# Query, key and value projections as three rounded products each, in an attention and expert kernel on one core

## The reference

```python
q = split_heads(layernorm(x) @ wq.T + bq)      # 16 heads of 16
k = split_heads(ctx @ wk.T + bk)
v = split_heads(ctx @ wv.T + bv)
attn = softmax(einsum('bhqd,bhkd->bhqk', q, k) / sqrt(16))
x = x + merge(attn @ v) @ wo.T + bo
n = layernorm(x)
probs = softmax((n @ Wg + bg) / 5.0)           # 8 experts
vals, idx = top_k(probs, 2); gates = mask / (sum(mask) + 1e-9)
h = gelu(n @ W1[e] + b1[e]); out_e = h @ W2[e] + b2[e]
x = x + sum_e gates[e] * out_e
```

## Time and profile before

| | |
|---|---|
| median of 3 runs | 808.66 us |
| profiled execution, whole | 804.46 us |
| its span, first to last instruction | 802.4 us |
| attention, batches 0 to 7 | 40.9 to about 524 us |
| expert tiles | about 524 to 802.4 us |
| batches 2 to 5 | about 62 us each |
| mean granted clock of PE, share of full speed | 0.992 |

### The profile page before, as it was taken

How to read it: one execution, slowest core, us unless ns; L and a number is a source line. 1 busy time by engine, 2 the same in 40 slices (tenths; PEclk the granted TensorE clock), 3 DMA queues, 4 the chain that set the end, 5 groups by cost and what they waited for, 6 DMA issues and landing times.

```text
span 802.4 us, 16337 instructions
## 1 busy us (share of the span) xinstructions
PE 755.2 (94%) x4672; PEld 451.9 (56%) x4672; DVE 612.2 (76%) x1126; ACT 455.1 (57%) x663; POOL 393.9 (49%) x357
## 2 busy tenths in 40 slices
PE   9999999999999999999999898869999999999994
PEld 4443344444444444444444333349989888999994
DVE  6787778798697787788788787667777887776773
ACT  2066676776766766766676674854345443444441
POOL 6506143547637728728725613306553564444443
PEclk9999999999999999999999999999999999999998
DMA  7665857657666767757658467666454465454441
GB/s 226 208 179 176 228 165 226 209 179 250 206 188 239 213 198 234 190 188 250 186 174 268 149 178 260 257 241 161 89 101 80 79 145 93 74 84 70 72 69 12
DMA packets 90660, 136.24 MB, mean 170 GB/s; under 512 B 15456, under 2 KB 49216, under 8 KB 90192
## 3 DMA queue, kind: packets, MB, share of 16 engines
q1 hardware_dynamic: 76592, 117.33, 48.0%
q0 software_dynamic: 13296, 17.09, 12.1%
q10 hardware_dynamic: 688, 0.79, 0.3%
HBM read 71.25 MB, written 64.04 MB: 169 GB/s over the span
## 4 chain that ended last, share of the span: by engine, by line
PE 71%; DMA 7%; DVE 7%; ACT 6%; issue 5%; SPq 2%; POOL 1%; POOLq 0%; DVEq 0%; another core or an unknown queue 0%
PE ps_pv L1568 13%; PE ring L1555 10%; PE ring L1734 9%; PE ring L1716 8%; PE ring L1542 7%; PE ps_x L1599 7%; ACT probs L1041 4%; PE ps_x L1619 4%; DMA out<-y_sb,xs 3%; PE ps_x L1609 3%; PE ring L1725 3%; DVE negm L1113 2%; PE ps_x L1629 2%; DMA den<-oT 2%; PE ps_pv L1707 1%
## 5 line engine op out<-in xcount | busy, mean ns | idle before, releaser
L1113 DVE TENSOR_REDUCE negm<-ring 128x2 f32<-128x1024 f32 x256 | 310.2, 1222 | 73.0 <-PE ring L1542 65.0
L1041 ACT ACTIVATE probs<-ring 128x1024 f32<-128x1024 f32 x256 | 260.0, 1024 | 91.7 <-PE ring L1555 79.4
L922 POOL DMA_INDIRECT out<-y_sb,xs x71 | 110.2, 1553 | 152.3 <-DMA out<-y_sb,xs 73.6
L1568 PE MATMUL ps_pv<-probs,v_aug 128*32 128x512 f32 x1024 | 136.8, 606 | 4.0 <-ACT probs L1041 3.9
L1555 PE MATMUL ring<-kq 64*128 64x512 f32 x512 | 125.4, 491 | 7.5 <-DVE negm L1113 7.3
L1542 PE MATMUL ring<-kq 64*128 64x512 f32 x512 | 105.9, 412 | 10.6 <-ACT probs L1041 5.4
L1555 PEld LDWEIGHTS ring<-kq 64*128 64x128 f32 x512 | 47.4, 183 | 108.5 <-issue 72.4
L1074 ACT CAST xsT_hi<-ps_pv 128x256 fp32r<-128x256 f32 x70 | 26.1, 373 | 133.8 <-PE ps_pv L1707 122.9
L1734 PE MATMUL ring<-w_hi,hT_hi 128*128 x284 | 85.3, 300 | 0.1
L815 POOL DMA_INDIRECT xs_dram<-xg,rows x64 | 63.3, 988 | 39.9 <-issue 15.9
L1734 PE MATMUL ring<-w_lo,hT_hi 128*128 x284 | 80.0, 282 | 0.0
(11 more groups left out here) (197 smaller groups left out, 1223.4 us busy)
## 6 DMA issues: line engine op xcount, KB each, us to landing
kq<-k_dram SPq DMA_DIRECT2D x64, 192.0 KB
kq<-q_dram SPq DMA_DIRECT2D x64, 192.0 KB
xs<-xs_dram SPq DMA_DIRECT2D x71, 132.5 KB
k_dram<-qk_hi SPq DMA_DIRECT2D x32, 256.0 KB
q_dram<-qk_hi SPq DMA_DIRECT2D x32, 256.0 KB, 2.8
o_dram<-oT SPq DMA_DIRECT2D x32, 256.0 KB
w_dram<-w_sb SPq DMA_DIRECT2D x12, 512.0 KB
w_hi<-w_dram SPq DMA_DIRECT2D x12, 512.0 KB, 7.4
```

The lines of the kernel that those rows point to most:

```text
L922: pool.indirect_dma_start(out=out, out_offset=bass.IndirectOffsetOnAxis(ap=xs[j % AHEAD][:, TOKEN:TOKEN + 1].bitcast(I32), axis=0), in_=y_ ...
L1041: nc.scalar.activation(probs[kt][:, 2 * jp:2 * jp + 2, :], ring[PLACE["ST", u, p] % RINGS][:], ACT.Exp).then_inc(exp_done, 1)
L1113: nc.vector.tensor_reduce(negm[:, v % 2, :, jp, kt], ring[PLACE["MX", v, p] % RINGS][:], AX.X, ALU.max, negate=True).then_inc(max_free, 1)
L1568: mm = nc.tensor.matmul(ps_pv[2 * DH * j:2 * DH * (j + 1), :], v_aug[:, kt, HPG * g + j, :], probs[kt][:, j, :], start=(kt == 0), stop=(kt ...
```

## The change

1. **Three rounded products.** For batches 1 to 7 every projection is `high*high + high*low + low*high` in float32r. Batch 0, which is projected ahead of the loops, stays float32.
2. **Who makes the parts.** ACT rounds the three weight matrices once. XT: ACT casts `ps_x` to `xn_hi` in place of the copy to xnT, then DVE takes `ps_x - xn_hi` to `xn_lo`, and only that frees the bank. Context: ACT rounds it in two halves (`high_kv`, rounds (3,3) and (3,4)), POOL takes the difference (`low_kv`).
3. **Memory.** The low parts lie over the whole ones, kvT has one buffer, the descriptor ring of POOL's transfers is 8192 in place of 16384 bytes a partition, and a scatter waits until the one two before it has landed.
4. **Moves.** XT0 of batch i+2 goes from round (2,7) to (2,6); the second staged cast from (3,2) to (3,5); the context load of batch i+2 on SP from the start of the batch to behind the weight load near its end; on POOL the first low part of a staged weight from ahead of the scatters to behind `ln2`, and Q1's split ahead of `ln`.

```diff
-NEXT = {(2, 7): "XT0", (3, 1): "XT1"}
+NEXT = {(2, 6): "XT0", (3, 1): "XT1"}
+XT_LOW = {(2, 7): "XT0", (3, 2): "XT1"}
+KV_HIGH = {(3, 3): 0, (3, 4): 1}
-STAGE_SLOTS = {(1, 2): 0, (3, 2): 1}
+STAGE_SLOTS = {(1, 2): 0, (3, 5): 1}
...
             def load_kv(b):
-                if b > 1:
-                    sp.wait_ge(full["V1"], b - 1)
-                sp.dma_start(kvT[:, b % 2], ctx_kv[b]).then_inc(kv_in, 16)
+                sp.wait_ge(full["V1"], b)
+                sp.dma_start(kvT[:], ctx_kv[b]).then_inc(kv_in, 16)
...
                 more = i + 1 < B
-                if i + 2 < B:
-                    load_kv(i + 2)
...
                 if i == 0:
                     load_w1(E - 2)
+                if i + 2 < B:
+                    load_kv(i + 2)
                 if more:
                     put_max(i + 1, 0)
...
+            def scatter_tile(b, k, t):
+                n = NT * (TOPK * b + k) + t
+                if n >= 2:
+                    pool.wait_ge(scattered[n % 2], 16 * (n // 2))
                 pool.indirect_dma_start(out=xs_dram, ...
+            def low_kv(b):
+                pool.wait_ge(kv_split, 3 * b - 1)
+                nc.gpsimd.tensor_tensor(kv_lo[:], kvT[:], kv_hi[:].bitcast(F32), ALU.subtract).then_inc(kv_split, 1)
...
                 if i + 1 < B:
                     split("K", i + 1, 0)
                     split("Q", i + 1, 0)
+                    split("Q", i + 1, 1)
                 if i + 2 < B:
                     ln(i + 2)
                 if i + 1 < B:
-                    split("Q", i + 1, 1)
                     split("K", i + 1, 1)
-                if i in STAGED:
-                    low_staged(i, 0)
                 if i > 1:
                     scatter(i - 2, NP * (NG * i + 1) + SCATTER if i < B - 1 else None)
                 if i > 0:
                     ln2(i - 1)
-                if i + 2 < B:
-                    add_bo(i + 2)
+                if i in STAGED:
+                    low_staged(i, 0)
                 if i + 1 < B:
                     for g in range(3):
                         place_v(i + 1, g)
+                if i + 2 < B:
+                    low_kv(i + 2)
+                    add_bo(i + 2)
                 if i in STAGED:
                     low_staged(i, 1)
...
-                if kind == "XT":
-                    if b > 0:
-                        act.wait_ge(full["Q1"], b)
+                if kind == "XT" and b == 0:
                     nc.scalar.copy(xnT[:, int(name[2]), :], ps[:]).then_inc(done[name], 1)
+                elif kind == "XT":
+                    nc.scalar.copy(xn_high(int(name[2])), ps[:].rearrange("p (t s) -> p t s", s=P)).then_inc(xt_high, 1)
...
+            def high_kv(b, c):
+                act.wait_ge(kv_in, 16 * (b + 1))
+                nc.scalar.copy(kv_hi[:, c, :], kvT[:, c, :]).then_inc(kv_split, 1)
...
+            for kind in "KQV":
+                whole_w, high, _ = w_parts[kind]
+                nc.scalar.copy(high[:], whole_w[:]).then_inc(w_split, 1)
             misc("MT", 0)
+            for c in range(DC):
+                high_kv(1, c)
...
+            def low_x(name, b):
+                c = int(name[2])
+                dve.wait_ge(xt_high, 2 * (b - 1) + c + 1)
+                dve.wait_ge(full["Q1"], b)
+                nc.vector.tensor_tensor(xn_lo[:, c, :]..., ps_x[:]..., xn_high(c).bitcast(F32), ALU.subtract).then_inc(done[name], 1)
...
+                        for c in range(DC):
+                            if name[0] == "Q":
+                                high = xn_high(c)[:, half.start // P:half.stop // P, :]
+                                low = xn_lo[:, c, half].rearrange("p (t s) -> p t s", s=P)
+                            else:
+                                high, low, res = kv_hi[:, c, half], kv_lo[:, c, half], ps[:, half]
+                            for n, (w, src) in enumerate(((w_hi, high), (w_hi, low), (w_lo, high))):
+                                mm = nc.tensor.matmul(res, w[:, c, f * P:(f + 1) * P], src, ...
...
+                            terms = [(x, w, c) for c in range(DC) for x, w in ((kv_hi, wv_hi), (kv_hi, wv_lo), (kv_lo, wv_hi))]
...
-    nc = bacc.Bacc("TRN2", target_bir_lowering=False, num_devices=1)
+    nc = bacc.Bacc("TRN2", target_bir_lowering=False, num_devices=1, dynamic_dma_scratch_size=8192)
```

More of the change, by code:

```diff
@@ L461, in w2_hi_free, with wait_scattered @@
                 eng.wait_ge(st_full, NP * (G - 1))
+        def wait_scattered(eng, b):
+            for n in range(2):
+                eng.wait_ge(scattered[n], 16 * TOPK * NT * b // 2)
         def stage_no(i, n):
@@ L904, in _ @@
                 place_v(0, g)
+            for n in range(3):
+                low_weights(n)
+            low_kv(1)
             add_bo(0)
```

130 lines of the change are left out of this document (90 added, 40 removed).

## The result

The kernel after takes 851.41 us, the median of 4 runs (848.17 to 855.31); the kernel before took 809.55 us beside it. The ratio is 1.054, with an interval of 1.050 to 1.058: 42 us slower, where 4 us less were forecast and the range ended at 812. The profiled execution spans 846.1 us, 43.7 more than the one before.

What follows compares the result with a forecast made beforehand. Attention was taken as paced by PE's own work. Batches 1 to 5 gain 2.8 us, batch 6 gains 1.8, batch 0 loses 0.35: 4.3 us less, 804.4 on the scale of the runs, range 794 to 812.

Steps and rivals of the forecast that it cites:

- the step on the scatters: POOL's scatters, two under way: eight take at most 20 us; 1 to 2 us more expected, covered by almost 5.
- The step beside it: POOL's Q1 split ahead of ln: put at nothing, because xn is wanted 20 us later.
- a smaller risk: Batch 7's unpaced scatters: in pairs of 5 us they would end 2 to 3 us late for ln2.
- I change no number for it: POOL sharing SBUF interfaces with DVE: no term, since DVE's long attention operations have at most one SBUF input.
- Rival 3: Context load near a batch's end lands late behind 512 KB of weights, ACT stalls 1.8 us; 6 us more, 815; 15%.
- The waits for the low parts: Batch 0: XT0 and XT1 of batch 1 each put 0.69 us on DVE before the next claim; 1.4 us.
- Rival 5: Standstill in round (2,2) of batches with scatters: the limit could remove it, five times 1.5, 7 us less, 797; 5%.
- The products: Projections on PE: rounded products shorten K and Q halves, Q1 and V units, saving 1.8 us a batch.
- that walk: Last rounds of a batch, from V1: moved and added ACT and DVE work costs 1.25 us, between 0.3 and 2.5.
- put at nothing: Edits given no cost because of cover: weight rounding, low_kv, Q1's split, staged low part, scatters, context load, smaller ring.
- 35%: Chance of the forecast itself, 4.3 us less than the profiled execution; half of it was counted as faster.
- rival 1: All of the gain arrives: ACT's and DVE's additions fit the ring's slack, or entry nears 0.08; 9 to 16 us less; 18%.

Runs made afterwards that it cites:

- e1: The kernel after without the limit of two scatters under way; 809.92 us, ratio 1.017.
- e2: The kernel after with ln ahead of Q1's split on POOL again, limit kept; 808.21 us, ratio 1.015.
- e5: The kernel after, unchanged, measured again in the second job; 847.21 us, ratio 1.065.
- e14: The kernel before with the limit of two scatters and Q1's split ahead of ln, large ring; 845.19 us, ratio 1.048.
- e4: The kernel before with the limit of two scatters alone; 814.63 us, ratio 1.024.
- e12: The kernel before with Q1's split ahead of ln on POOL, scatters not limited; 825.83 us, ratio 1.025.
- e13: e12 with the descriptor ring of half the size; 828.04 us, ratio 1.026.
- e15: The kernel of e1 again, in the fourth job; 832.59 us, ratio 1.032.
- e7: e3 with POOL's bias addition and first staged low part back where they were, the second behind V's last group in the next batch; 802.71 us, ratio 1.008.
- e9: e8 with the second staged low part on POOL behind the split of Q0 in the next batch; 801.19 us, ratio 0.996.
- e3: The kernel after without the limit and with ln ahead of Q1's split; 807.08 us, ratio 1.017.
- e8: e7 with SP issuing the context load ahead of the store of the reciprocal; 797.72 us, ratio 1.003.
- e6: The kernel before, unchanged, profiled in the second job; 799.68 us in one run.
- e10: e4 with the descriptor ring of half the size; 811.6 us, ratio 1.006.
- e11: e4 with the first staged low part on POOL behind ln2, so that scatters start sooner; 840.54 us, ratio 1.046.
- e16: The kernel before, unchanged, profiled in the fourth job; 805.87 us.

## Why the prediction was wrong

**The step that failed** is the one on the scatters: "a landing takes at most 5.0 us. Eight scatters in pairs then take at most 4 x 5 = 20 us, were every landing that slow; I expect 1 to 2 more, since XG0 follows `ln2` by almost 5 us." Two errors are in it. The bound came from the landing of one scatter in a kernel without the limit; under the limit the four pairs of batch 3 took 4.6, 6.8, 5.8 and 8.2 us, and the eight scatters 25.5. And even the 20 of the bound is 4 more than the 16.3 of before, not 1 to 2; for those a pair would have to take 4.3 to 4.6 us.

**The step beside it** took the cover twice. "Q1's split ahead of `ln`: xn is wanted 20 us later" names what needs xn, but not what stands behind that wait on POOL: the scatters and `ln2`, whose slack of 4 to 5 us the step on the scatters had already counted as its own. 5 us of later start and 9 of slower landings meet one slack of 4. In batches 2 to 5, undone one at a time (e1, e2), either fits; together they stall in the kernel after (e5) and in the kernel before (e14). The sum had no rival with both in it. Neither edit is free alone: the limit alone makes XG0 wait 0.5 to 2.8 us a batch in e4 and 4 us in batch 7 of e2 and e4, which the prediction had named as a smaller risk, "2 to 3 us late"; the order alone brings standstills of 3 to 8 us a batch (e12, e13), and so does the kernel after without the limit in e15.

**The half clock** was in no term. After 6 to 10 us without work PE came back at a granted clock of 0.50 and stayed there for 4 to 6 us, which made round (3,4) 1.4 to 1.8 us longer in each of the four batches.

**What POOL does beside DVE.** "I change no number for it", the prediction said on this. Here it costs 0.7 us in (0,0), 0.4 in (0,1) (e7) and most of 1.1 in (0,6), which e9 takes out, about 2 us a batch, since `low_kv`, the bias and a staged low part were moved to where DVE multiplies numT. The Trainium skill (GPSIMD Engine Reference, Key points) names both cases: contention "with DVE instructions in a 2-port perf mode or with two SBUF inputs". The traces agree for two inputs (numT 2.68, `pr` 0.87), and give the size: DVE ends a fixed time behind POOL's instruction, so it waits out the whole of it. That `veps`, with one input, is held up as well (1.39) fits the first case; no run showed its mode. The prediction looked at the long operations only and missed one of 0.69 us at the wrong place.

**What takes half of the gain.** In (1,4) 0.8 us of the 1.7 that the products save is lost again, in e3 as in e7, e8 and e9: in e3 PE waits there 1.2 us for a reduction of DVE, which stands behind small routing operations, among them `row_k`, which ends with POOL's split of Q1. It is long in the kernel before too (1.01 us in e6, 1.11 in e3, 0.19 alone), but there it ends 0.1 us into the round and in e3 0.8. What makes it later against PE's rounds was not tested. No term of the sum had DVE in the rounds of the projections.

**Rival 3**, the late context, came true in batch 0 alone: issued at 91.7, landed at 100.2, ACT idle for 2.57. In batches 2 to 5 the larger stall covered it; batch 4 of e1 showed it once more (2.7 us). Batch 0 as a whole, forecast 0.35 us longer, lost 6.5: 4.1 in (3,5) to (3,7) by the context and the half clock behind it, 2.9 in (0,5) to (0,7) by XT1's low part, for which PE waited 1.35 us, and the half clock again. The waits for the low parts were in the sum (1.4 us), the late context was only in a rival, and the half clock behind either was in neither.

**Rival 5** was right in its mechanism: under the limit no trace shows the standstill, not even where the same order without it loses 3 to 8 us a batch (e14 against e12, and against e13 in its own job). Its chance had nothing to do with the main loss. But it explains most of why the ratio is 1.054 in the first measurement and 1.065 in e5: the change costs 42 and 51 us, and of the 9 between them some 6 are standstills in batches 2 to 6 of the kernel before, which had none in the job of e5. "Ended by no engine of this core" was a reading of the view: by the semaphore events these waits end with a late signal of PE, in batch 4 at 321.91 for an ST pair whose row ended at 320.34.

**What was right.** The products: a K half 320.33 - 319.42 = 0.91, Q1 330.18 - 328.59 = 1.59, V1 357.60 - 355.97 = 1.63, forecast 0.91, 1.58 and 1.63. In e3 the rounds with projections are 1.7 us a batch shorter than in e6 (forecast 1.8). Rounds (2,6) to (3,7) are 1.0 us longer there (forecast 1.25), and the MX pair of (3,0) waits 0.8 us for ACT, as the walk had it; XG0 waits 0.26 for DVE's low part, forecast 0.35. The bounds of that walk, 0.3 to 2.5, held; the terms that decided stood in the list of edits "put at nothing". One sum beside the time is off: half of 35% with the 18% of rival 1 and the 5% of rival 5 makes 0.405 for faster, not 0.43.

**Not settled.** Batch 7 and the expert tiles take about 3.6 us less in the kernel after (first pair, and e5 against e6) with the same work in the tiles. And in a standstill ACT, DVE and POOL wait for late signals of PE; whether PE's products themselves stop or only their signals come late, and what of the scatters does it, the traces do not say, since the ends of PE's rows are modelled.

## What to carry to other kernels

When an edit makes an engine wait, write down the queue behind it, and the slack of the first reader in that queue; then book all edits that delay this queue against that one slack together, not each against the whole of it. Under a limit, transfers last (number / limit) x the time of one round of landings, taken under load and not from one landing in a kernel without the limit; here issues followed each other every 1.26 us and a pair took 4.6 to 8.2, so two under way made 19 to 26 us of the eight in batch 3, where without a limit they took 12 to 17. And when work is moved on POOL, look at what DVE does at the new time: an operation of 0.2 to 0.7 us there can wait for the whole of POOL's instruction.

## What the runs showed of the hardware

- A stop of PE, ACT and DVE while POOL issues indirect scatters without a pause: 1.1 to 1.6 us a batch in the kernel before in two of three profiles and none in the third, 2.7 to 7.6 in e12, gone with at most two scatters under way (e10 and e11 beside e9 and e12; e14 beside e13, e15 and e16; e4 says nothing on it, since no kernel of its job has the stop). Each such wait of ACT and DVE ends with a signal of PE that comes late, in batch 3 of e12 by 5.5 us. In e12 the DMA engines were at 1.00 and 312 GB/s in the 5 us before. The same kernel has it in one job and not in another (e15, e1). The half ring does not remove it (e13).
- A DVE operation with two inputs from SBUF that meets a POOL operation waits for its end and doesn't share: numT 2.68 us in place of 0.69, beside a POOL instruction of 2.38 that had begun 0.25 before it. `veps`, with one input, waited too (1.39 in place of 0.17), while DVE's reduction from PSUM did not: in batch 4 of e3 it took 1.23 us beside a POOL operation of 1.26 us, as it does alone.
- The half clock can follow a short wait too. In batch 0 of the kernel after PE waited 1.35 us and, behind one transpose, 0.34 more; the granted clock from 51.9 to 55.1 was 0.50, and products of 256 columns followed each other at 0.21 us, elsewhere at 0.12 (PE's timeline):

```profile
51.21 0.28 PE L1658 MATMUL ps_x<-ident,negm 128*16 128x128 f32 x1 [1.35 <-DVE xn_lo L1226]
51.83 0.58 PE L1696 MATMUL ps_x<-kv_hi,wk_hi 128*128 128x256 f32 x1 [0.34 <-ACT mT L1042]
52.21 0.41 PE L1696 MATMUL ps_x<-kv_lo,wk_hi 128*128 128x256 f32 x1
52.42 0.41 PE L1696 MATMUL ps_x<-kv_hi,wk_lo 128*128 128x256 f32 x1
```
